# One attention layer of a four-layer graph network: attended products put off by two pairs and placed beside the scores

## The chip, the core and the metric

The kernel runs on one core of a Trainium2 chip. TensorE (PE in the profile, PEld for its weight loads), VectorE (DVE), ScalarE (ACT), GpSimd (POOL) and SyncE (SP) each run their own program and meet at semaphores. The metric is the device time of one launch in microseconds; lower is better.

## The reference

Input x is 64 graphs of 128 nodes with 256 features, with one 128x128 adjacency. Four layers follow, each x = x + layer(relu(layernorm(x))). The change touches the last, a masked attention of 8 heads of 32 features:

```python
q = (x @ Wq + bq).reshape(b, n, H, HD)      # likewise k, v
scores = jnp.einsum('bqhd,bkhd->bhqk', q, k) / jnp.sqrt(jnp.float32(HD))
scores = scores + (1.0 - adj)[None, None, :, :] * -1000000000.0
attn = jax.nn.softmax(scores, axis=-1)
out = jnp.einsum('bhqk,bkhd->bqhd', attn, v).reshape(b, n, d)
return out @ Wo + bo
```

## The kernel before

All of x stays in SBUF. The 64 graphs are worked on as 32 pairs (PAIRS = 32), layer after layer. In the last layer every engine runs a list of steps named period(p); the lists are software pipelines written out by hand, so a step of one pair stands beside steps of the pairs next to it, and the order of the calls in period is the order on the engine. A head belongs to one of R = 4 row groups r (32 features) and one of C = 2 chunks c, so a group r holds four 128x128 score blocks of a pair: two graphs by two chunks.

What happens to pair p, with its lines:

- PE turn: transposes the normalised x (L143). ACT relu_high (L1167) and DVE low_h (L1278) split its ReLU in a high and a low part.
- PE project_q, project_k, project_v: 12 matmuls each (L365). ACT copy_q (L1173), DVE copy_k (L1254) and copy_v (L1261) bring the results to SBUF. The projections of k and v land in the PSUM banks of score groups 0 and 1, so scores waits for both copies.
- PE scores (L1096): 16 matmuls with 32 rows of contraction, four groups of rows; the trace counts two passes of each.
- DVE mask_max(p, r) (L1267 and L1270): adds the mask, takes the negated maximum. ACT exponentials(p, r) (L1181): four instructions with their sums. DVE inverse(p, r) (L1274), POOL divide(p, r) (L1233).
- PE turn_prob(p, r) (L1104): four transposes into one of two banks PT; ACT copy_pT (L1188) brings them to probT.
- PE attend (L1114): 16 matmuls with full contraction and 32 columns of output, into bank OT. ACT copy_o (L1193) makes the high part, DVE low_o (L1283) the low part. PE project_o (L365 with wo), whose result YY is the same bank as OT. DVE update (L1290) adds it to x, SP stores the pair (L1341).
- Statistics for pair p + 3: DVE moments, mean_variance (L107, L114) and root_argument (nmean L120, vare L121); POOL inverse_root and centre (L132, L336). POOL add_bias (L1228) adds the output bias to x.

attend(p - 1) stands in period p behind project_k, project_o(p - 2) behind scores. On DVE, update(p - 2) stands early in the period, behind low_h; at the end come copy_v(p + 1), root_argument, low_o(p - 1). Waits that matter here: attend(p) needs all four copy_pT of its pair and update(p - 1) (x_done); scores(p) needs v_ready of pair p; low_o needs copy_o; project_o needs low_o. The loops run two pairs a turn on PE and DVE, one on ACT.

Of the kernel before, what the change touches and what calls it, by code (L numbers as in the profile page):

```python
# [14 lines left out]
def gnn_stack_kernel(nc, x, adj, w):  # L15


    GRAPHS, N, D = x.shape
    PAIRS = GRAPHS // 2
# [10 lines left out]
    with ExitStack() as ctx:  # L30
        def sb(name, shape, dt=F32):
            return ctx.enter_context(nc.sbuf_tensor(name, shape, dt))
# [52 lines left out]
        prob = sb("prob", [128, R, 2 * C, N])  # L85
        probT = sb("probT", [128, R, 2 * C, N])
        qT = sb("qT", [128, C, 2, N])
# [297 lines left out]
        with nc.Block() as block:  # L385
# [671 lines left out]
            QUAD = 2 * C  # L1057
            valb = [val, val1]
            nmax = [small[:, QUAD * r:QUAD * (r + 1)] for r in range(R)]
# [3 lines left out]
            def has(p, low, high=PAIRS):  # L1063
                return not isinstance(p, int) or low <= p < high

            @block.tensor
            def _(pe):
                def turn(p, b):
                    pe.wait_ge(xn_ready, p + 1)
                    pe.wait_ge(q_ready, since(p))  # L1070
                    transposes(TQ, xnb[b]).then_inc(tr_done, 1)

# [34 lines left out]
                def attend(p, b):  # L1107
                    pe.wait_ge(pt_ready, R * p + R)
                    pe.wait_ge(x_done, since(p))
                    for g in range(2):  # L1110
                        for c in range(C):
                            for r in range(R):
                                h = c * R + r
                                ins = nc.tensor.matmul(OT[HD * r:HD * (r + 1), (g * C + c) * N:(g * C + c + 1) * N],  # L1114
                                                       valb[b][:, g, HD * h:HD * (h + 1)], probT[:, r, g * C + c, :],
                                                       start=True, stop=True)
                    ins.then_inc(o_done, 1)
# [8 lines left out]
                def period(p, b):  # L1126
                    if has(p, 0):
                        scores(p)
                    if has(p, 2, PAIRS + 2):
                        project_o(p - 2)  # L1130
                    if has(p, 1, PAIRS + 1):
                        turn_prob(p - 1, 2)
                        turn_prob(p - 1, 3)
                    if has(p, 0, PAIRS - 1):
                        project_q(p + 1)
                        project_k(p + 1)
                    if has(p, 1, PAIRS + 1):
                        attend(p - 1, 1 - b)
                    if has(p, 0):
                        turn_prob(p, 0)  # L1140
                    if has(p, 0, PAIRS - 1):
                        project_v(p + 1)
                    if has(p, 0, PAIRS - 2):
                        turn(p + 2, b)
                    if has(p, 0):
                        turn_prob(p, 1)
# [6 lines left out]
                pe.wait_ge(l2_x_done, PAIRS)  # L1153
                period(0, 0)
                period(1, 1)
                with pe.Fori(1, PAIRS // 2 - 1) as j:
                    period(2 * j, 0)
                    period(2 * j + 1, 1)
                for p in range(PAIRS - 2, PAIRS + 2):
                    period(p, p % 2)  # L1160

            @block.scalar
            def _(act):
# [20 lines left out]

                def copy_pT(p, r):
                    act.wait_ge(pt_done, R * p + r + 1)
                    act.wait_ge(o_done, since(p))
                    nc.scalar.copy(probT[:, r, :, :].rearrange("p i n -> p (i n)"), PT[r % 2][:, :]).then_inc(pt_ready, 1)  # L1188

# [4 lines left out]

                def period(p):
                    if has(p, 1, PAIRS + 1):
                        copy_pT(p - 1, 1)
                    if has(p, 0, PAIRS - 1):
                        relu_high(p + 1)
                    if has(p, 0):  # L1200
                        exponentials(p, 0)
                    if has(p, 1, PAIRS + 1):
                        copy_pT(p - 1, 2)
                        copy_pT(p - 1, 3)
                    if has(p, 0):
                        exponentials(p, 1)
                    if has(p, 0, PAIRS - 1):
                        copy_q(p + 1)
                    if has(p, 0):
                        exponentials(p, 2)  # L1210
                    if has(p, 1, PAIRS + 1):
                        copy_o(p - 1)
                    if has(p, 0):
                        copy_pT(p, 0)
                        exponentials(p, 3)

                copy_q(0)
                period(0)
                with act.Fori(1, PAIRS - 1) as p:
                    period(p)  # L1220
                period(PAIRS - 1)
                period(PAIRS)

# [26 lines left out]
            def _(dve):  # L1250
# [7 lines left out]
                def copy_v(p, b):  # L1258
                    dve.wait_ge(v_done, p + 1)
                    dve.wait_ge(o_done, since(p - 1))  # L1260
                    nc.vector.tensor_tensor(valb[b][:, :, 0:D], VV[:, :].rearrange("p (g d) -> p g d", g=2),  # L1261
                                            rows[:, 1:2, :].to_broadcast([128, 2, D]), ALU.add).then_inc(v_ready, 1)
# [30 lines left out]
                def period(p, b):  # L1293
# [4 lines left out]
                    if has(p, 0, PAIRS - 1):  # L1298
                        low_h(p + 1)
                    if has(p, 2, PAIRS + 2):  # L1300
                        update(p - 2)
                    if has(p, 0):
                        mask_max(p, 1)
                        inverse(p, 0)
                        mask_max(p, 2)
                    if has(p, 0, PAIRS - 1):
# [4 lines left out]
                    if has(p, 0, PAIRS - 3):  # L1311
                        dve.wait_ge(xn_ready, p + 2)
                        moments(dve, p + 3, dstep, 1 - b)
                        mean_variance(dve, p + 3, dstep, 1 - b)
                    if has(p, 0):
                        inverse(p, 2)
                    if has(p, 0, PAIRS - 1):
                        copy_v(p + 1, 1 - b)
                    if has(p, 0, PAIRS - 3):
                        root_argument(dve, p + 3, dstep, stats_ready, 1 - b)  # L1320
                    if has(p, 1, PAIRS + 1):
                        low_o(p - 1)

# [3 lines left out]
                layer_norm_stats(dve, 2, dstep, stats_ready, 0)  # L1327
                period(0, 0)
                period(1, 1)
                with dve.Fori(1, PAIRS // 2 - 2) as j:  # L1330
                    period(2 * j, 0)
                    period(2 * j + 1, 1)
                for p in range(PAIRS - 4, PAIRS + 2):
                    period(p, p % 2)

# [31 lines left out]
```

## Time and profile before

| | us |
|---|---|
| median of 3 runs | 810.2 (810.06 to 811.39) |
| the profiled execution | 807.73 |
| its span, first to last instruction | 805.5 |
| busy: PE, DVE, ACT, POOL | 747.7, 716.3, 592.6, 491.5 |
| mean granted TensorE clock | 0.987 of full |

The time of the profiled execution is the span and 2.2 us around it. The last layer begins at about 450 us. In its steady part PE, DVE and ACT are all over nine tenths busy, so the page alone doesn't say which sets the pace; the waits and the order in time do. In the timeline a row gives the start, the length, the engine, the line, what it writes and reads, how many instructions were merged, and in brackets how long the engine was idle before it and what ended that.

### The profile page before, as it was taken

The page shows a single profiled execution, that of the slowest core. Times are in us where ns is not written, and L with a number is a line of the kernel's source. Part 1 is how long each engine was busy: PE and PEld are TensorE (multiplying, and loading weights), DVE is VectorE, ACT ScalarE, POOL GpSimd, SP SyncE. Part 2 cuts the span into 40 slices and gives each one's busy share as a digit, 9 for nine tenths or more (in the row PEclk, how much of TensorE's full clock was granted, in tenths as well). Part 3 has the DMA queues.
Part 4 walks back from the last instruction along what each step waited for, and adds up shares of the span by engine and source line. Part 5 has one row for each costly group of instructions (what it writes and reads, how often), then busy time and mean ns, then how long its engine had stood idle before and what let it go on. Part 6 is the DMA issues. An engine that isn't in the chain of part 4 may idle for free.

```text
span 805.5 us, 23074 instructions
## 1 busy us (share of the span) xinstructions
PE 747.7 (93%) x7065; PEld 684.9 (85%) x7065; DVE 716.3 (89%) x1941; ACT 592.6 (74%) x1928; POOL 491.5 (61%) x615
## 2 busy tenths in 40 slices
PE   4999999998889888887999889999999999999995
PEld 3899999998667666666999779999999999999994
DVE  4688888886899999998999889999999999999984
ACT  2544555454877887875766489999999999999995
POOL 1355545554566666667888466666667666666653
PEclk8999999999999999999999999999999999999998
DMA  6333300000000000000000000000000000000001
GB/s 192 92 92 91 91 0 0 0 0 0 2 1 0 0 0 0 0 1 1 1 0 0 1 15 27 25 15 26 26 26 26 26 26 26 26 13 26 26 28 39
DMA packets 21642, 19.91 MB, mean 25 GB/s; under 512 B 2416, under 2 KB 21616, under 8 KB 21616
## 3 DMA queue, kind: packets, MB, share of 16 engines
q1 hardware_dynamic: 19440, 18.16, 7.2%
q10 hardware_dynamic: 2176, 1.44, 0.6%
q8 instruction: 11, 0.18, 0.1%
q14 instruction: 15, 0.12, 0.1%
HBM read 11.21 MB, written 8.39 MB: 24 GB/s over the span
## 4 chain that ended last, share of the span: by engine, by line
PE 33%; ACT 28%; DVE 17%; issue 11%; POOL 8%; ACTq 1%; DVEq 0%; POOLq 0%
ACT prob L1181 20%; PE bank L365 18%; ACT probT L1188 5%; POOL xs L801 5%; PE bank L417 3%; PE bank L430 3%; DVE stats L107 3%; PE bank L345 3%; DVE wide L1267 3%; DVE small L1270 3%; POOL rstd L132 3%; PE bank L143 2%; DVE tT L840 2%; PE bank L425 1%; DVE prob L845 1%
## 5 line engine op out<-in xcount | busy, mean ns | idle before, releaser
L1181 ACT ACTIVATE prob<-wide,small 128x128 f32<-128x128 f32 x512 | 199.5, 395 | 27.2 <-DVE small L1270 27.2
L1233 POOL TENSOR_TENSOR prob<-prob,small 128x512 f32<-128x512 f32 x128 | 133.2, 1041 | 109.3 <-DVE small L1274 107.4
L132 POOL TENSOR_TENSOR rstd<-vare,mhalf 128x2 f32<-128x2 f32 x128 | 88.8, 694 | 99.5 <-DVE vare L121 99.5
L107 DVE BATCH_NORM_STATS2 stats<-xs 128x6 f32 (+1 forms) x256 | 95.2, 413 | 7.9 <-DMA xs<-in_x_dram 5.0
L1181 ACT ACTIVATION_READ_ACCUMULATOR prob<-wide,small 128x1 f32 x512 | 98.4, 192 | 0.0
L1270 DVE TENSOR_REDUCE small<-wide 128x4 f32<-128x512 f32 x128 | 87.8, 686 | 4.4
L1267 DVE TENSOR_TENSOR wide<-bank,mbias 128x512 f32<-128x512 f32 x128 | 86.1, 672 | 1.3 <-PE bank L1096 1.0
L329 ACT ACTIVATE xn<-xs,shift,rstd 128x256 f32 (+1 forms) x128 | 70.3, 601 | 16.2 <-POOL shift L138 16.2
L1104 PE MATMUL bank<-ident,prob 128*128 128x128 f32 x512 | 74.4, 279 | 1.2 <-POOL prob L1233 1.2
L1188 ACT COPY probT<-bank 128x512 f32<-128x512 f32 x128 | 70.7, 576 | 1.7 <-PE bank L1104 1.7
L1104 PEld LDWEIGHTS bank<-ident,prob 128*128 128x128 f32 x512 | 58.0, 142 | 7.8 <-issue 6.1
L355 PE MATMUL bank<-w,hT 128*128 128x257 f32 x256 | 62.5, 387 | 0.8 <-ACT hT L724 0.8
L143 PE MATMUL bank<-ident,xn 128*128 128x128 f32 x384 | 58.0, 274 | 0.5 <-DVE xn L1031 0.5
L365 PE MATMUL bank<-hTs,wq 128*128 128x256 f32 x384 | 54.2, 290 | 3.1 <-DVE hTs L1278 3.1
L365 PE MATMUL bank<-wo,oTs 128*128 128x256 f32 x384 | 54.9, 292 | 2.2 <-DVE oTs L1283 2.2
L355 PEld LDWEIGHTS bank<-w,hT 128*128 128x128 f32 x256 | 49.3, 194 | 8.8 <-ACT hT L724 1.3
L365 PE MATMUL bank<-w,yTs 128*128 128x256 f32 x384 | 54.1, 290 | 1.8 <-DVE xs L998 1.1
L519 POOL TENSOR_TENSOR relsq<-relm 128x256 f32<-128x256 f32 x32 | 22.1, 689 | 54.2 <-PE bank L430 54.2
L365 PE MATMUL bank<-wv0T,hTs 128*128 128x256 f32 x384 | 53.9, 289 | 1.1 <-DVE oTs L579 1.1
L365 PE MATMUL bank<-hTs,m_qk 128*128 128x256 f32 x384 | 52.4, 286 | 2.5 <-PEq L189 1.9
L365 PEld LDWEIGHTS bank<-wo,oTs 128*128 128x128 f32 x384 | 48.1, 190 | 6.3 <-DVE oTs L1283 2.7
L365 PE MATMUL bank<-wv,hTs 128*128 128x256 f32 x384 | 53.2, 287 | 0.0
(132 smaller groups left out, 1969.6 us busy)
## 6 DMA issues: line engine op xcount, KB each, us to landing
out_dram<-xs SPq DMA_DIRECT2D x32, 256.0 KB, 2.1
xs<-in_x_dram SPq DMA_DIRECT2D x28, 256.0 KB, 2.7
xs<-in_x_dram ACTq DMA_DIRECT2D x1, 768.0 KB, 7.6
xs<-in_x_dram ACTq DMA_DIRECT2D x1, 256.0 KB, 4.2
wq<-in_L_gnn_Wq_dram SPq DMA_DIRECT2D x1, 256.0 KB, 3.9
wk<-in_L_gnn_Wk_dram SPq DMA_DIRECT2D x1, 256.0 KB, 4.6
wv<-in_L_gnn_Wv_dram SPq DMA_DIRECT2D x1, 256.0 KB, 7.3
w<-in_L_gnn_W_dram SPq DMA_DIRECT2D x1, 256.0 KB, 8.2
```

The lines of the kernel that those rows point to most:

```text
L107: ins = nc.vector.bn_stats(stats[:, b, g, :], x_of(p, g))
L132: nc.gpsimd.tensor_tensor(rstd[:, b, :], vare[:, b, :], mhalf[:, :], ALU.pow).then_inc(rstd_ready, 1)
L143: ins = nc.tensor.transpose(pe_ps[:, c * 2 * N + g * N:c * 2 * N + (g + 1) * N], src[:, g, c * 128:(c + 1) * 128], ident[:, :])
L329: ins = nc.scalar.activation(dst[:, g, :], x_of(p, g), ACT.Relu, bias=shift[:, b, g:g + 1], scale=rstd[:, b, g:g + 1])
L355: ins = nc.tensor.matmul(ps_g, hT[:, c, g, :], weight[:, c, :], start=(c == 0), stop=(c == C - 1))
L365: ins = nc.tensor.matmul(ps, lhsT(a, c), rhs(b, c), start=(n == 0), stop=(n == len(terms) - 1))
L1104: ins = nc.tensor.transpose(PT[r % 2][:, i * N:(i + 1) * N], prob[:, r, i, :], ident[:, :])
L1181: ins = nc.scalar.activation(prob[:, r, i, :], wide[:, r, i, :], ACT.Exp, bias=nmax[r][:, i:i + 1], accum_out=rsum[r][:, i:i + 1])
L1188: nc.scalar.copy(probT[:, r, :, :].rearrange("p i n -> p (i n)"), PT[r % 2][:, :]).then_inc(pt_ready, 1)
L1233: nc.gpsimd.tensor_tensor(prob[:, r, :, :], prob[:, r, :, :], rinv[r].unsqueeze(2).to_broadcast([128, QUAD, N]), ALU.mult).then_inc(prob_r ...
L1267: nc.vector.tensor_tensor(wide[:, r, :, :], SS[r][:, :].rearrange("p (i n) -> p i n", i=QUAD), mbias_quad, ALU.add).then_inc(s_masked, 1)
L1270: nc.vector.tensor_reduce(nmax[r], wide[:, r, :, :], AX_X, ALU.max, negate=True).then_inc(nmax_ready, 1)
```

## The change

- attend(p - 2) now stands in period p directly behind scores(p); project_o(p - 2) moves behind project_k(p + 1).
- probT gets two buffers, the values four (val2, val3 are added); copy_pT waits for the attended products of one pair earlier, copy_v of two pairs earlier than before.
- ACT: copy_o(p - 2) stands behind exponentials(p, 0); before, copy_o(p - 1) stood behind exponentials(p, 2).
- DVE: low_o(p - 2) stands behind inverse(p, 0), update(p - 2) near the end; root_argument and update now stand ahead of copy_v(p + 1), which is last.
- The loops run four pairs a turn on PE and DVE, two on ACT.

No instruction of arithmetic is added or taken away. The diff, without the loop headers:

```diff
@@ -83,7 +83,8 @@
         rnorm = sb("rnorm", [128, 2])
         wide = sb("wide", [128, R, 2 * C, N])
         prob = sb("prob", [128, R, 2 * C, N])
-        probT = sb("probT", [128, R, 2 * C, N])
+        probT = [sb(f"probT{b}", [128, R, 2 * C, N]) for b in range(2)]
+        val2, val3 = sb("val2", [128, 2, D + 1]), sb("val3", [128, 2, D + 1])
         qT = sb("qT", [128, C, 2, N])
         kT = sb("kT", [128, C, 2, N])
         small = sb("small", [128, 64])
...
@@ -1055,7 +1056,7 @@
             SS, PT, OT, TQ = bank[0:4], bank[4:6], bank[6], bank[7]
             KK, VV, YY = SS[0], SS[1], OT
             QUAD = 2 * C
-            valb = [val, val1]
+            valb = [val, val1, val2, val3]
             nmax = [small[:, QUAD * r:QUAD * (r + 1)] for r in range(R)]
             rsum = [small[:, 16 + QUAD * r:16 + QUAD * (r + 1)] for r in range(R)]
             rinv = [small[:, 32 + QUAD * r:32 + QUAD * (r + 1)] for r in range(R)]
...
@@ -1112,7 +1113,7 @@
                             for r in range(R):
                                 h = c * R + r
                                 ins = nc.tensor.matmul(OT[HD * r:HD * (r + 1), (g * C + c) * N:(g * C + c + 1) * N],
-                                                       valb[b][:, g, HD * h:HD * (h + 1)], probT[:, r, g * C + c, :],
+                                                       valb[b][:, g, HD * h:HD * (h + 1)], probT[b % 2][:, r, g * C + c, :],
                                                        start=True, stop=True)
                     ins.then_inc(o_done, 1)
 
...
@@ -1127,15 +1128,15 @@
                     if has(p, 0):
                         scores(p)
                     if has(p, 2, PAIRS + 2):
-                        project_o(p - 2)
+                        attend(p - 2, (b + 2) % 4)
                     if has(p, 1, PAIRS + 1):
                         turn_prob(p - 1, 2)
                         turn_prob(p - 1, 3)
                     if has(p, 0, PAIRS - 1):
                         project_q(p + 1)
                         project_k(p + 1)
-                    if has(p, 1, PAIRS + 1):
-                        attend(p - 1, 1 - b)
+                    if has(p, 2, PAIRS + 2):
+                        project_o(p - 2)
                     if has(p, 0):
                         turn_prob(p, 0)
                     if has(p, 0, PAIRS - 1):
...
@@ -1182,44 +1183,45 @@
                                                    accum_out=rsum[r][:, i:i + 1])
                     ins.then_inc(exp_done, 1)
 
-                def copy_pT(p, r):
+                def copy_pT(p, r, b):
                     act.wait_ge(pt_done, R * p + r + 1)
-                    act.wait_ge(o_done, since(p))
-                    nc.scalar.copy(probT[:, r, :, :].rearrange("p i n -> p (i n)"), PT[r % 2][:, :]).then_inc(pt_ready, 1)
+                    act.wait_ge(o_done, since(p - 1))
+                    nc.scalar.copy(probT[b][:, r, :, :].rearrange("p i n -> p (i n)"), PT[r % 2][:, :]).then_inc(pt_ready, 1)
 
                 def copy_o(p):
                     act.wait_ge(o_done, p + 1)
                     act.wait_ge(y_done, since(p))
                     nc.scalar.copy(oTs[0][:, :, :, :].rearrange("p g c n -> p (g c n)"), OT[:, :]).then_inc(o_high_ready, 1)
 
-                def period(p):
+                def period(p, b):
                     if has(p, 1, PAIRS + 1):
-                        copy_pT(p - 1, 1)
+                        copy_pT(p - 1, 1, 1 - b)
                     if has(p, 0, PAIRS - 1):
                         relu_high(p + 1)
                     if has(p, 0):
                         exponentials(p, 0)
+                    if has(p, 2, PAIRS + 2):
+                        copy_o(p - 2)
                     if has(p, 1, PAIRS + 1):
-                        copy_pT(p - 1, 2)
-                        copy_pT(p - 1, 3)
+                        copy_pT(p - 1, 2, 1 - b)
+                        copy_pT(p - 1, 3, 1 - b)
                     if has(p, 0):
                         exponentials(p, 1)
                     if has(p, 0, PAIRS - 1):
                         copy_q(p + 1)
                     if has(p, 0):
                         exponentials(p, 2)
-                    if has(p, 1, PAIRS + 1):
-                        copy_o(p - 1)
-                    if has(p, 0):
-                        copy_pT(p, 0)
+                        copy_pT(p, 0, b)
                         exponentials(p, 3)
 
...
@@ -1257,7 +1259,7 @@
 
                 def copy_v(p, b):
                     dve.wait_ge(v_done, p + 1)
-                    dve.wait_ge(o_done, since(p - 1))
+                    dve.wait_ge(o_done, since(p - 3))
                     nc.vector.tensor_tensor(valb[b][:, :, 0:D], VV[:, :].rearrange("p (g d) -> p g d", g=2),
                                             rows[:, 1:2, :].to_broadcast([128, 2, D]), ALU.add).then_inc(v_ready, 1)
 
...
@@ -1297,11 +1299,12 @@
                         mask_max(p, 0)
                     if has(p, 0, PAIRS - 1):
                         low_h(p + 1)
-                    if has(p, 2, PAIRS + 2):
-                        update(p - 2)
                     if has(p, 0):
                         mask_max(p, 1)
                         inverse(p, 0)
+                    if has(p, 2, PAIRS + 2):
+                        low_o(p - 2)
+                    if has(p, 0):
                         mask_max(p, 2)
                     if has(p, 0, PAIRS - 1):
                         copy_k(p + 1)
...
@@ -1310,28 +1313,28 @@
                         mask_max(p, 3)
                     if has(p, 0, PAIRS - 3):
                         dve.wait_ge(xn_ready, p + 2)
-                        moments(dve, p + 3, dstep, 1 - b)
-                        mean_variance(dve, p + 3, dstep, 1 - b)
+                        moments(dve, p + 3, dstep, 1 - b % 2)
+                        mean_variance(dve, p + 3, dstep, 1 - b % 2)
                     if has(p, 0):
                         inverse(p, 2)
+                    if has(p, 0, PAIRS - 3):
+                        root_argument(dve, p + 3, dstep, stats_ready, 1 - b % 2)
+                    if has(p, 2, PAIRS + 2):
+                        update(p - 2)
                     if has(p, 0, PAIRS - 1):
-                        copy_v(p + 1, 1 - b)
-                    if has(p, 0, PAIRS - 3):
-                        root_argument(dve, p + 3, dstep, stats_ready, 1 - b)
-                    if has(p, 1, PAIRS + 1):
-                        low_o(p - 1)
+                        copy_v(p + 1, (b + 1) % 4)
 
```

## Rows read from the trace of the kernel before

**Rows 1.** Waits in 470 to 780 us: who waited for what, us in total, times, longest

```profile
ACT prob L1181 <- DVE small L1270: 21.6, 29, 0.8
...
DVE small L1274 <- ACT prob L1181: 9.8, 30, 0.9
```

**Rows 2.** Timeline of one pair, VectorE (start us, length us, engine, line, operation)

```profile
646.83 0.69 DVE L1267 TENSOR_TENSOR wide<-bank,mbias 128x512 f32<-128x512 f32 x1
...
648.15 0.68 DVE L1278 SCALAR_TENSOR_TENSOR hTs<-bank,hTs 128x512 fp32r<-128x512 f32 x1
...
648.75 0.68 DVE L1290 TENSOR_TENSOR xs<-bank,xs 128x512 f32 x1
...
650.75 0.66 DVE L1267 TENSOR_TENSOR wide<-bank,mbias 128x512 f32<-128x512 f32 x1
...
655.06 0.14 DVE L1274 RECIPROCAL small<-small 128x4 f32<-128x4 f32 x1
...
655.12 0.68 DVE L1261 TENSOR_TENSOR val<-bank,rows 128x512 f32<-128x512 f32 x1
...
655.71 0.64 DVE L120 TENSOR_SCALAR nmean<-mv 128x2 f32<-128x2 f32 x1
...
657.42 0.69 DVE L1267 TENSOR_TENSOR wide<-bank,mbias 128x512 f32<-128x512 f32 x1
```

**Rows 3.** Timeline of the same pair, ScalarE

```profile
648.35 0.40 ACT L1181 ACTIVATE prob<-wide,small 128x128 f32<-128x128 f32 x1 [0.79 <-DVE small L1270]
...
649.91 1.04 ACT L1188 COPY probT<-bank 128x512 f32<-128x512 f32 x2
...
654.58 0.19 ACT L1181 ACTIVATION_READ_ACCUMULATOR prob<-wide,small 128x1 f32 x1
```

**Rows 4.** Timeline of the same pair, TensorE

```profile
648.89 1.70 PE L365 MATMUL bank<-hTs,wq 128*128 128x256 f32 x12
...
650.42 1.60 PE L365 MATMUL bank<-hTs,wk 128*128 128x256 f32 x12
...
652.96 0.42 PEld L1104 LDWEIGHTS bank<-ident,prob 128*128 128x128 f32 x4 [0.20 <-issue]
...
656.01 1.01 PEld L1096 LDWEIGHTS bank<-kT,qT 32*128 32x128 f32 x32 [0.32 <-issue]
```

**Rows 5.** Timeline of pair 0 to 1: copy_v, scores, mask_max

```profile
463.76 0.66 DVE L1261 TENSOR_TENSOR val<-bank,rows 128x512 f32<-128x512 f32 x1
...
464.65 1.01 PEld L1096 LDWEIGHTS bank<-kT,qT 32*128 32x128 f32 x32 [1.49 <-issue]
...
464.68 1.17 PE L1096 MATMUL bank<-kT,qT 32*128 32x128 f32 x32 [1.28 <-DVE val L1261]
...
465.91 0.69 DVE L1267 TENSOR_TENSOR wide<-bank,mbias 128x512 f32<-128x512 f32 x1 [0.78 <-PE bank L1096]
```

**Rows 6.** Timeline of the same pair as group 2, GpSimd

```profile
653.91 1.30 POOL L1228 TENSOR_TENSOR xs<-xs,rows 128x512 f32<-128x512 f32 x1
...
655.28 1.04 POOL L1233 TENSOR_TENSOR prob<-prob,small 128x512 f32<-128x512 f32 x1
```

**Rows 7.** Timeline of the last pairs and the end

```profile
783.44 1.17 PE L1096 MATMUL bank<-kT,qT 32*128 32x128 f32 x32 [0.55 <-DVE val L1261]
...
797.79 1.08 PE L1114 MATMUL bank<-probT,val 128*32 128x128 f32 x32 [0.67 <-ACT probT L1188]
...
798.93 0.58 ACT L1193 CAST oTs<-bank 128x512 fp32r<-128x512 f32 x1 [1.20 <-PE bank L1114]
...
799.55 0.69 DVE L1283 TENSOR_TENSOR oTs<-bank,oTs 128x512 fp32r<-128x512 f32 x1 [3.42 <-ACT oTs L1193]
...
802.04 0.69 DVE L1290 TENSOR_TENSOR xs<-bank,xs 128x512 f32<-128x512 f32 x1 [1.79 <-PE bank L365]
```

**Rows 8.** Lines 120 and 121: durations ns min/median/max, first and last start

```profile
L120 DVE TENSOR_SCALAR nmean<-mv x128: 152/224/655, 6.1 to 762.0; 128x2 f32<-128x2 f32 x128
...
L121 DVE TENSOR_SCALAR vare<-mv x128: 152/155/164, 6.2 to 762.6; 128x2 f32<-128x2 f32 x128
```

More of the change, by code:

```diff
@@ L1070, in turn @@
                     pe.wait_ge(q_ready, since(p))
-                    transposes(TQ, xnb[b]).then_inc(tr_done, 1)
+                    transposes(TQ, xnb[b % 2]).then_inc(tr_done, 1)
                 def project_q(p):
@@ L1153, in _ @@
                 pe.wait_ge(l2_x_done, PAIRS)
[L1154 to L1160, printed above, removed]
+                for p in range(4):
+                    period(p, p)
+                with pe.Fori(1, PAIRS // 4 - 1) as j:
+                    for i in range(4):
+                        period(4 * j + i, i)
+                for p in range(PAIRS - 4, PAIRS + 2):
+                    period(p, p % 4)
             @block.scalar
@@ L1210, in period @@
                         exponentials(p, 2)
-                    if has(p, 1, PAIRS + 1):
-                        copy_o(p - 1)
-                    if has(p, 0):
-                        copy_pT(p, 0)
+                        copy_pT(p, 0, b)
                         exponentials(p, 3)
                 copy_q(0)
[L1218 to L1222, printed above, removed]
+                period(0, 0)
+                period(1, 1)
+                with act.Fori(1, PAIRS // 2 - 1) as j:
+                    period(2 * j, 0)
+                    period(2 * j + 1, 1)
+                for p in range(PAIRS - 2, PAIRS + 2):
+                    period(p, p % 2)
             @block.gpsimd
@@ L1327, in _ @@
                 layer_norm_stats(dve, 2, dstep, stats_ready, 0)
[L1328 to L1332, printed above, removed]
+                for p in range(4):
+                    period(p, p)
+                with dve.Fori(1, PAIRS // 4 - 1) as j:
+                    for i in range(4):
+                        period(4 * j + i, i)
                 for p in range(PAIRS - 4, PAIRS + 2):
-                    period(p, p % 2)
+                    period(p, p % 4)
             @block.sync
```

## The prediction

> **What bounds the kernel now.** I read three views, in this order. First the table of waits over the steady stretch of the last layer [rows 1]: the only two waits that recur once a pair are the exponentials on ACT for the negated maximum from DVE (29 times, 21.6 us, so 0.74 us a pair) and the reciprocals on DVE for the exponentials (30 times, 9.8 us). ACT and DVE wait for each other; nobody is shown waiting for PE, although PE is as full as they are. Then the timeline of one pair [rows 2 to 4]. I call m the start of mask_max(p, 0). One pair lasts 657.42 - 646.83 = 10.59 us there [rows 2], and the mean over 30 pairs, from scores(1) at 464.68 (its weight load is in [rows 5]) to scores(31) at 783.44 [rows 7], is 10.63 us. The circle is: the last exponential of a pair ends, DVE can take inverse(p-1, 3), then mask_max(p, 0); ACT starts exp 0 at m + 1.52 (648.35 - 646.83) [rows 2, 3] and is then full to the end of the pair.
>
> Last, the second circle, which no table names: copy_v, scores, mask_max. copy_v starts at 655.12 and runs about 0.67 us, so it ends near 655.8, and the scores' weight load starts at 656.01 [rows 2, 4]. The row puts 0.32 us of idle down to "issue". But in pair 1 the same load is idle 1.49 us, and it starts 0.89 us after copy_v's start (463.76 to 464.65) [rows 5], as it does here (655.12 to 656.01). PE had nothing else left there, so it waits for v_ready in both; the wait is real and stands hidden in "issue". From copy_v's start to the next mask_max is 2.15 us when nothing else holds it (463.76 to 465.91) [rows 5]. In the steady pair copy_v starts at m + 8.29 [rows 2], so this circle is 8.29 + 2.15 = 10.44 us long against the real 10.59. Its slack is 0.15 us. Any delay of copy_v beyond that lengthens every pair.
>
> **The change part by part.** *PE.* attend (1.0 us: project_k starts at 650.42, a projection takes 1.53 to the next, and the transposes behind attend load at 652.96 [rows 4]) moves up behind scores; project_o (12 matmuls, like project_q, so 1.53) moves down behind project_k. project_q waits for low_h: 648.15 + 0.68 = 648.83, q at 648.89 [rows 2, 4], so it can't start earlier. Hence the stretch from q to the last transposes grows by some 0.5 us less what a change of array shape costs. PE was through with its other loads at 656.01 - 0.32 = 655.69, i.e. m + 8.9, and would be at m + 9.4. This is under the m + 10.3 found below, so it costs nothing, and what PE saves gives nothing either. For the shapes: the weight load after attend is idle 0.20 us [rows 4]; of four changes of shape a pair one goes, since the scores (32 rows) and the attended products (32 columns) are themselves two shapes. I price that at 0 to 0.3 us a pair on PE, hidden.
>
> The Trainium skill (TensorEngine Tiling (Array Packing), Key Properties) says that a change of tiling mode, not merely of tile, drains the array. The 0.20 us agree. By that rule alone the change would give 0.20 x 30 = 6 us if PE set the time; it is the first rival below.
>
> *ACT.* copy_o(p-2) goes between exp 0 and the copies of turned probabilities, the same instruction, none added. It starts no earlier than m + 1.52 + (649.91 - 648.35) = m + 3.08 and lasts 0.57 (798.93) [rows 3, 7], so it ends at m + 3.65. Its own input, attend, ends before m + 1. Exp 2 then ends at most 0.57 later than before relative to exp 0: m + 1.52 + (654.58 + 0.19 - 648.35) + 0.57 = m + 8.51.
>
> *DVE.* Here is the cost. (a) low_o takes update's place early in the pair. They are alike (PSUM and SBUF in, 512 wide; from one such operation to the next takes 0.60, as low_h to update [rows 2]), so the exchange is free, but low_o now needs copy_o. DVE reaches it at m + 3.32 (650.75 - 646.83 less 0.60) [rows 2]; copy_o ends at m + 3.65 and low_o follows 0.05 later (798.93 + 0.57 = 799.50, then 799.55) [rows 7]. So DVE stands 0.37 us, and behind it are queued mask_max 2, copy_k, mask_max 3 and all the rest. (b) update moves in front of copy_v: 0.60 us (copy_v to the next is 0.59 [rows 2]). (c) root_argument moves in front of copy_v. It costs 0.59 + more where it stands now, since nmean lasts 0.64 us instead of 0.15; its end, 656.35, is that of divide on POOL, 655.28 + 1.04 = 656.32 [rows 2, 6]. At the new place, 0.06 us behind inverse(p, 2), the divide which that reciprocal releases has not begun (POOL starts 0.22 behind it). Free, two such small operations cost 0.14 us (0.06 to 0.08 each to the next; shortest durations 0.15 in [rows 8]). Bounds 0.14 and 1.1 (a whole divide first); I take 0.14. (d) The waits ahead of inverse(p, 2): DVE reaches it at m + 8.23 + 0.37 = 8.60, behind exp 2's 8.51, so it adds nothing.
>
> Copy_v now starts at m + 8.29 + 0.37 + 0.14 + 0.60 = m + 9.40; project_v is over by then (q at m + 2.06, three projections 1.53 apart, four transposes of 0.42 together, a fourth projection and its tail of 0.2: m + 8.8, from [rows 4]). With 2.15 for copy_v, scores and the way to mask_max the pair is **11.55 us** instead of 10.63: +0.92. The old cover is gone: root_argument, low_o and inverse 3 used to run on DVE during the scores; now only inverse 3 does, and DVE and ACT both stand while the scores run.
>
> *Buffers.* The second probT and four values relax waits on o_done that show in no table; worth nothing here.
>
> *Sum.* Pairs 2 to 28: 27 x 0.92 = 24.9 us. Pairs 29 and 30 have no statistics; there exp 2 holds inverse(p, 2) until m + 8.5, and the pair is 8.5 + 0.1 + 0.6 + 2.15 = 11.3, some 0.7 more: 1.3 us. Pairs 0 and 1 have no low_o or update: only root_argument, 0.3 us. *The end:* now 18.6 us pass from scores(31) to the last update, and 4.25 from attend(31) to it [rows 7]. With the lag, attend(31) must wait for update(30), and that for the whole line attend, copy_o, low_o, project_o of pair 30, which itself waits for project_o behind turn_prob(31, 3). Laying these in line gives update(30) at 13.4 to 14.0 after the last m, attend(31) at 14.25 and update(31) at 18.5 against 17.2: +1.3 us (bounds 0 and 3). In all 24.9 + 1.3 + 0.3 + 1.3 = 27.8 us. The profiled execution took 807.7 us and would take 835.5. The median of the runs is 0.3% above the profiled one, so I give 810.2 + 27.8 = **838 us**.
>
> Bounds of the terms: without the 0.37 us the sum falls by 10 us, so 828; rounding in the six small steps is 2 us, so 826. With root_argument held for a whole divide in each pair, +1.0 x 28 = 28 us, so 866.
>
> **Rivals.** *PE is the bound (faster).* PE is idle for only some tenths of a us a pair, and its 0.32 us before scores and 0.20 after attend could both be changes of shape. Then three instead of four save 0.20 us x 30 = 6 us: 804. It decides if scores don't wait for copy_v. Against it: the 1.49 us of idle at the same place, with the same 0.89 us behind copy_v [rows 5]. Chance 0.06.
>
> *The ACT and DVE circle absorbs it (no change).* If DVE still reached mask_max before the last exponential was through, the pair would stay 10.6 and the time 810 to 812. It needs copy_v to be at most 0.15 us later; the instructions put before it come to 1.1 us. Chance 0.05.
>
> *POOL gets in ahead of root_argument (slower still).* The margin is small: add_bias (653.91 + 1.30 = 655.21 [rows 6], so m + 8.38, with the 0.37 m + 8.75) still runs when nmean comes at m + 8.66, and the divide can start at m + 8.82. If the divide slips in before vare, update and copy_v wait 1.0 us more: 12.6 us a pair, 866. For it: nmean held today. Against: vare never took over 0.164 us in 128 [rows 8]. Chance 0.14. The Trainium skill (SBUF — State Buffer, Who interferes with whom) says that a VectorE tensor_scalar in a two-port mode and a GpSimd instruction exclude each other for a whole instruction, whoever comes first. By that rule nmean ahead of the divide is free; behind it the 866 holds. The 656.35 against 656.32 agrees.
>
> **How the numbers follow.** My case, slower by 3.4%, has 0.75. The range 826 to 866 takes in all slower cases and leaves out the two others, 0.11, and some error of the sum. A difference under about 0.2% can't be told from none by a measurement of this kernel. Faster 0.06, same 0.05, slower 0.89.
>
> **What would show it.** Right: in the steady pairs DVE is idle before mask_max(p, 0) for roughly 1 us, released by the scores on PE (L1096), and ACT before exp 0 for about 1.5 us; DVE is idle before low_o 0.3 to 0.4 us, released by copy_o; nmean is short; PE is idle before scores some 0.8 us behind copy_v; scores to scores is 11.5 us. Wrong: scores start long after copy_v's end, or nmean or vare lasts over 0.6 us at the new place, or DVE still waits for exp 3 and not for scores.

## The result

The changed kernel is slower: median 845.2 us (6 runs) against 810.8 us of the kernel before (6 runs), a ratio of 1.0418 with a 95% interval of 1.0389 to 1.0447. That is 34 us, where 27.8 were forecast; 838 was named and 826 to 866 was the range. One of the six runs of the changed kernel took 1207 us at a granted clock of 0.557; the ratio leaves it out, and the median of the other five is 845.1 us. The profiled execution took 847.4 us, its span is 845.7 us.

The changed kernel's lines are one or two higher than before: scores L1097, attend L1115, copy_o L1194, copy_v L1263, mask_max L1269 and L1272, low_o L1285, update L1292, exponentials L1182, reciprocals L1276. Its table of waits over the steady part of the last layer (who waited for whom, us in total, times, longest) answers [rows 1]:

```profile
PEld bank L1097 <- issue: 39.2, 29, 2.3
DVE wide L1269 <- PE bank L1097: 34.0, 30, 1.5
PE bank L1097 <- DVE val L1263: 33.0, 29, 2.0
PEld bank L366 <- DVE hTs L1280: 13.2, 30, 1.3
...
DVE small L1276 <- ACT prob L1182: 8.6, 29, 0.8
```

Two new waits stand near the top that before had not: DVE's mask_max for the scores (30 times, 34.0 us) and the scores for copy_v (29 times, 33.0 us). They are the two halves of one circle. The timeline of one pair, VectorE, answers [rows 2]; m is now 646.85:

```profile
646.85 0.69 DVE L1269 TENSOR_TENSOR wide<-bank,mbias 128x512 f32<-128x512 f32 x1 [1.15 <-PE bank L1097]
...
648.18 0.68 DVE L1280 SCALAR_TENSOR_TENSOR hTs<-bank,hTs 128x512 fp32r<-128x512 f32 x1
...
650.53 0.69 DVE L1285 TENSOR_TENSOR oTs<-bank,oTs 128x512 fp32r<-128x512 f32 x1 [0.27 <-ACT oTs L1194]
651.14 0.68 DVE L1269 TENSOR_TENSOR wide<-bank,mbias 128x512 f32<-128x512 f32 x1
...
655.46 0.15 DVE L1276 RECIPROCAL small<-small 128x4 f32<-128x4 f32 x1
...
655.59 0.17 DVE L121 TENSOR_SCALAR nmean<-mv 128x2 f32<-128x2 f32 x1
...
655.66 0.17 DVE L122 TENSOR_SCALAR vare<-mv 128x2 f32<-128x2 f32 x1
...
655.80 0.69 DVE L1292 TENSOR_TENSOR xs<-bank,xs 128x512 f32 x1
...
656.41 0.68 DVE L1263 TENSOR_TENSOR val<-bank,rows 128x512 f32<-128x512 f32 x1
...
657.32 0.18 DVE L1276 RECIPROCAL small<-small 128x4 f32<-128x4 f32 x1 [0.23 <-ACT prob L1182]
...
658.68 0.69 DVE L1269 TENSOR_TENSOR wide<-bank,mbias 128x512 f32<-128x512 f32 x1 [1.18 <-PE bank L1097]
```

The same pair on TensorE and ScalarE, for [rows 3, 4]:

```profile
647.62 0.86 PEld L1105 LDWEIGHTS bank<-ident,prob 128*128 128x128 f32 x8 [0.20 <-issue]
...
648.37 0.40 ACT L1182 ACTIVATE prob<-wide,small 128x128 f32<-128x128 f32 x1 [1.92 <-PE bank L1105]
...
648.91 1.49 PEld L366 LDWEIGHTS bank<-hTs,wq 128*128 128x128 f32 x12 [0.43 <-DVE hTs L1280]
...
649.93 0.57 ACT L1194 CAST oTs<-bank 128x512 fp32r<-128x512 f32 x1
...
657.32 1.01 PEld L1097 LDWEIGHTS bank<-kT,qT 32*128 32x128 f32 x32 [1.36 <-issue]
...
657.35 1.17 PE L1097 MATMUL bank<-kT,qT 32*128 32x128 f32 x32 [1.15 <-DVE val L1263]
...
658.45 0.81 PEld L1115 LDWEIGHTS bank<-probT,val 128*32 128x32 f32 x32
```

The pair lasts 658.68 - 646.85 = 11.83 us, against 10.59 in [rows 2]. copy_v starts at m + 9.56 (it was 8.29); low_o waits 0.27 us for copy_o; VectorE stands 1.18 us before mask_max, TensorE's weight loads 1.36 us before the scores. ScalarE's wait before exp 0, put down to TensorE here, is 1.92 us where it was 0.79 [rows 3].

Where the 40.2 us between the two spans lie, by the starts of the scores: up to scores(0), in code that did not change, 2.3 us (454.23 to 456.57); pair 0, 1.7 us (10.45 to 12.18); pairs 1 to 30, 34.1 us (10.63 to 11.76 on average); from scores(31) to the last update 2.1 us (18.6 to 20.7). In pair 0 TensorE stands 2.1 us for low_h, and 0.6 us behind the end of this its clock falls to the lower level of 1.2 GHz. Two stretches of the changed kernel (busy time of each engine with count, then the granted clock, before the DMA's share):

```profile
459.90:464.30 4.40, 4.40 (x24) 4.40 (x25) 2.54 (x5) 4.13 (x21) 1.04 (x1) 0.61 0.00 0
...
839.20:842.20 3.00, 2.91 (x12) 2.62 (x12) 0.03 (x1) 0.00 (x0) 0.00 (x0) 0.52 0.00 0
```

project_q and project_k of pair 1 took 2.47 and 2.38 us there, against 1.70 and 1.60 at the full clock. The second stretch is the last project_o: 2.91 us instead of 1.70. The fall in pair 0 does not come with the new order: of the 12 profiled executions behind this document it is missing in that of the kernel before alone, and e5 below, in which only VectorE's order differs from before, has it. The end of the kernel before has a stretch at half clock of its own:

```profile
462.10:465.50 3.40, 3.40 (x19) 3.40 (x17) 1.65 (x4) 3.14 (x16) 1.04 (x1) 0.50 0.00 0
```

```profile
794.10:797.50 3.40, 3.01 (x15) 2.61 (x13) 0.87 (x2) 1.73 (x5) 1.04 (x1) 0.50 0.07 24
```

The first is e5 in pair 0, the second the kernel before in its last pairs. The profiled execution of before (807.7 us) was also shorter than each of its six runs of this comparison, and that of the changed kernel the longest of its five. That is the likely reason why the spans differ by 40 and the medians by 34, but the other executions have no trace that would show it.

### The profile page after: what moved, and what is told of

Same layout as the page of the kernel before. It is cut to its first block, busy times and chain, and to the rows that moved or that the text cites. A ratio compares the mean times of both kernels' runs of the same rounds, so it can differ in the third digit from the quotient of the medians.

```text
span 845.7 us, 22865 instructions
## 1 busy us (share of the span) xinstructions
PE 751.2 (89%) x7065; PEld 687.1 (81%) x7065; DVE 711.2 (84%) x1941; ACT 592.5 (70%) x1928; POOL 491.1 (58%) x615
## 4 chain that ended last, share of the span: by engine, by line
PE 36%; DVE 29%; issue 13%; POOL 10%; ACT 8%; DVEq 1%; ACTq 0%; POOLq 0%
PE bank L366 18%; DVE wide L1269 7%; ACT prob L1182 6%; DVE stats L108 5%; PE bank L1097 5%; POOL xs L802 4%; PE bank L418 3%; DVE small L1272 3%; PE bank L431 3%; PE bank L346 3%; DVE val L1263 3%; POOL rstd L133 2%; DVE kT L1256 2%; ACT oTs L1194 2%; PE bank L144 2%
## 5 line engine op out<-in xcount | busy, mean ns | idle before, releaser
L1182 ACT ACTIVATE prob<-wide,small 128x128 f32<-128x128 f32 x512 | 200.2, 400 | 63.5 <-PE bank L1105 47.5
L1269 DVE TENSOR_TENSOR wide<-bank,mbias 128x512 f32<-128x512 f32 x128 | 87.1, 681 | 34.9 <-PE bank L1097 34.9
L1182 ACT ACTIVATION_READ_ACCUMULATOR prob<-wide,small 128x1 f32 x512 | 101.4, 198 | 0.0
L1272 DVE TENSOR_REDUCE small<-wide 128x4 f32<-128x512 f32 x128 | 87.8, 686 | 4.4
L1097 PE MATMUL bank<-kT,qT 32*128 32x128 f32 x1024 | 37.6, 282 | 36.1 <-DVE val L1263 36.1
L1097 PEld LDWEIGHTS bank<-kT,qT 32*128 32x128 f32 x1024 | 32.2, 186 | 42.9 <-issue 42.9
L366 PEld LDWEIGHTS bank<-hTs,wq 128*128 128x128 f32 x384 | 48.4, 191 | 15.5 <-DVE hTs L1280 15.5
L366 PE MATMUL bank<-wo,oTs 128*128 128x256 f32 x384 | 52.7, 287 | 3.8 <-DVE oTs L1285 3.8
```

What stands on the lines that cost most here:

```text
L366: ins = nc.tensor.matmul(ps, lhsT(a, c), rhs(b, c), start=(n == 0), stop=(n == len(terms) - 1))
L1097: ins = nc.tensor.matmul(SS[r][:, (g * C + c) * N:(g * C + c + 1) * N], qT[rows_r, c, g, :], kT[rows_r, c, g, :], start=True, stop=True)
L1182: ins = nc.scalar.activation(prob[:, r, i, :], wide[:, r, i, :], ACT.Exp, bias=nmax[r][:, i:i + 1], accum_out=rsum[r][:, i:i + 1])
L1269: nc.vector.tensor_tensor(wide[:, r, :, :], SS[r][:, :].rearrange("p (i n) -> p i n", i=QUAD), mbias_quad, ALU.add).then_inc(s_masked, 1)
L1272: nc.vector.tensor_reduce(nmax[r], wide[:, r, :, :], AX_X, ALU.max, negate=True).then_inc(nmax_ready, 1)
```

## The experiments

Two theories. **A**, that of the prediction: copy_v comes late on VectorE, the scores wait for it, and mask_max for the scores; the order on VectorE costs the time. **B**: TensorE's new order costs it, project_q standing for low_h (0.4 us a pair in the table of waits) and project_o ahead of project_v. All edits are in the last layer; "pair" is the mean from scores(1) to scores(31) of the profiled execution.

| run | median us | ratio to before, 95% | pair us |
|---|---|---|---|
| before | 810.8 | | 10.63 |
| changed | 845.2 | 1.039 to 1.045 | 11.76 |
| e1_copyv_first | 818.3 | 1.007 to 1.012 | 10.91 |
| e2_update_late | 826.2 | 1.018 to 1.022 | 11.13 |
| e3_root_late | 838.3 | 1.031 to 1.036 | 11.56 |
| e4_lowo_late | 846.5 | 1.043 to 1.047 | 11.76 |
| e5_before_copyv_last | 832.2 | 1.023 to 1.029 | 11.37 |
| e6_attend_first | 855.3 | 1.053 to 1.057 | 12.07 |
| e8_v_early_split | 809.9 | 0.998 to 1.002 | 10.65 |
| e9_v_early_only | 809.3 | 0.996 to 0.999 | 10.61 |
| e10_loop_unrolled | 839.0 | 1.032 to 1.037 | 11.60 |
| e12_lag_tuned | 815.3 | 1.002 to 1.007 | 10.80 |

### Undoing the order on VectorE, step by step

```diff
 # e1_copyv_first, in VectorE's period of the changed kernel
                         inverse(p, 2)
+                    if has(p, 0, PAIRS - 1):
+                        copy_v(p + 1, (b + 1) % 4)
                     if has(p, 0, PAIRS - 3):
                         root_argument(dve, p + 3, dstep, stats_ready, 1 - b % 2)
                     if has(p, 2, PAIRS + 2):
                         update(p - 2)
-                    if has(p, 0, PAIRS - 1):
-                        copy_v(p + 1, (b + 1) % 4)
```

> The changed kernel with one edit: on VectorE copy_v(p+1) stands directly behind inverse(p,2) again, ahead of root_argument and update. TensorE, ScalarE, lag and buffers stay as changed. Theory A (the time is lost because copy_v comes late and scores wait for it): copy_v starts at m + 8.7 and the way to the next mask_max takes 2.2 to 2.3, so a pair takes 10.9 to 11.0 us instead of 11.8 and the time is 818 to 822 us. Rival B (the time is lost in TensorE's new order: project_q waits for low_h, and project_o stands ahead of project_v): the order on VectorE hardly matters, over 838 us.

Measured 818.3 us, as A has it. Theory B is out for the bulk of the loss: TensorE's order, the lag and the buffers are all still there, and 27 of the 34 us are gone. The 7 or 8 us left are the changed kernel's rest. Timeline of this kernel, one pair:

```profile
642.77 0.69 DVE L1269 TENSOR_TENSOR wide<-bank,mbias 128x512 f32<-128x512 f32 x1 [0.27 <-PE bank L1097]
...
646.45 0.69 DVE L1285 TENSOR_TENSOR oTs<-bank,oTs 128x512 fp32r<-128x512 f32 x1 [0.26 <-ACT oTs L1194]
...
651.45 0.66 DVE L1263 TENSOR_TENSOR val<-bank,rows 128x512 f32<-128x512 f32 x1
...
652.02 0.65 DVE L121 TENSOR_SCALAR nmean<-mv 128x2 f32<-128x2 f32 x1
...
652.33 1.01 PEld L1097 LDWEIGHTS bank<-kT,qT 32*128 32x128 f32 x32 [0.43 <-issue]
...
653.69 0.69 DVE L1269 TENSOR_TENSOR wide<-bank,mbias 128x512 f32<-128x512 f32 x1 [0.27 <-PE bank L1097]
```

copy_v starts at m + 8.68 (651.45 - 642.77) and mask_max 2.24 us behind it: the same circle still holds the pair, at 10.92 us. It is 0.39 us later than in [rows 2], about as much as low_o's wait for copy_o pushes the steps behind it (in the changed kernel mask_max 2 starts at m + 4.29, in [rows 2] at m + 3.92). And nmean is back at 0.65 us: behind a copy_v it meets the divide on GpSimd again.

```diff
 # e2_update_late; here and in e3 the conditions ahead of the calls are left out
                         root_argument(dve, p + 3, dstep, stats_ready, 1 - b % 2)
-                        update(p - 2)
                         copy_v(p + 1, (b + 1) % 4)
+                        update(p - 2)
 # e3_root_late
-                        root_argument(dve, p + 3, dstep, stats_ready, 1 - b % 2)
                         update(p - 2)
                         copy_v(p + 1, (b + 1) % 4)
+                        root_argument(dve, p + 3, dstep, stats_ready, 1 - b % 2)
```

> The changed kernel with one edit: update(p-2) stands behind copy_v instead of ahead of it; root_argument stays ahead. Theory A: 0.61 to 0.68 us off in each of 29 pairs, 18 to 20 us, so 825 to 828 us. Rival B: within 3 us of the changed kernel, 842 to 846.

> The changed kernel with one edit: root_argument stands behind copy_v instead of ahead of it; update stays ahead. Theory A: root_argument costs 0.2 us a pair where it stands, 27 pairs, so 5 us are won, 840 us; nmean then runs into the divide on POOL again, but in the shadow of the scores. A rival in which nmean is held for a whole divide at the changed place would win 15 us or more here, under 832.

Measured 826.2 and 838.3 us. Update's place is worth 0.63 us a pair (11.76 - 11.13), root_argument's 0.20 (11.76 - 11.56), together 0.83, and e1 has 0.85: the two add, as two steps in a row on one path do. The rival in which nmean is held for a whole divide is out.

```diff
 # e4_lowo_late
-                    if has(p, 2, PAIRS + 2):
-                        low_o(p - 2)
                     if has(p, 0):
                         mask_max(p, 2)
+                    if has(p, 2, PAIRS + 2):
+                        low_o(p - 2)
```

> The changed kernel with one edit: low_o(p-2) stands behind mask_max(p,2) instead of ahead of it, where copy_o is long done. Theory A: VectorE's wait of 0.35 us for copy_o goes in each of 29 pairs, 10 us, so 835 us; project_o starts 0.3 us later, which may take a part of it back by a later project_v. Rival: the wait is hidden behind another (exp 2 or project_v), then 843 to 846.

Measured 846.5 us: nothing is won, and the rival in it was right, though it named other waits. VectorE in that kernel (copy_k, the reciprocal of group 1, the mask of group 3):

```profile
650.16 0.69 DVE L1256 TENSOR_TENSOR kT<-bank,bk 128x512 f32<-128x512 f32 x1
651.11 0.18 DVE L1276 RECIPROCAL small<-small 128x4 f32<-128x4 f32 x1 [0.26 <-ACT prob L1182]
651.20 0.68 DVE L1269 TENSOR_TENSOR wide<-bank,mbias 128x512 f32<-128x512 f32 x1
```

The step from copy_k to the mask was 0.68 us in the changed kernel and is 1.04 here (651.20 - 650.16), with inverse(p, 1) standing for exp 1. Exp 1 ends where it did, at m + 6.16 in both kernels, and copy_o stands ahead of it on ScalarE; in the kernel before, without copy_o there, it ends at m + 5.7. So I put the 0.36 us down to copy_o's place on ScalarE: low_o's wait was only the first one to show it, and taken away it turns up 2.5 us later as another.

### Doing it alone, on the kernel before

```diff
 # e5_before_copyv_last, on the kernel before
-                    if has(p, 0, PAIRS - 1):
-                        copy_v(p + 1, 1 - b)
                     if has(p, 0, PAIRS - 3):
                         root_argument(dve, p + 3, dstep, stats_ready, 1 - b)
                     if has(p, 1, PAIRS + 1):
                         low_o(p - 1)
+                    if has(p, 0, PAIRS - 1):
+                        copy_v(p + 1, 1 - b)
```

> The kernel before with one edit: on VectorE copy_v(p+1) stands last in the period, behind root_argument and low_o(p-1). No lag, no new buffer, TensorE and ScalarE as before. Theory A: copy_v starts at m + 9.1 instead of 8.3, a pair takes 11.3 us instead of 10.6, and the time is 828 to 833 us: most of the change's loss without the change. Rival B (TensorE's order): within 3 us of before, 808 to 814.

Measured 832.2 us. Without any lag, buffer or new order on TensorE, the late copy_v alone costs 22 us, at 0.74 us a pair.

### Is the shared stretch worth anything on TensorE?

```diff
 # e6_attend_first, in TensorE's period of the changed kernel
+                    if has(p, 2, PAIRS + 2):
+                        attend(p - 2, (b + 2) % 4)
                     if has(p, 0):
                         scores(p)
-                    if has(p, 2, PAIRS + 2):
-                        attend(p - 2, (b + 2) % 4)
```

> The changed kernel with one edit: attend(p-2) stands ahead of scores(p) instead of behind it, so it runs while TensorE waits for copy_v. Theory A: TensorE is not what sets the pair, 843 to 847 us, the pair stays 11.8; the idle time ahead of scores shrinks by 1 us and that ahead of project_q grows by as much. Rival C (the order of the two shapes of the array matters for the time): more than 4 us either way.

Measured 855.3 us, 10 slower than the changed kernel. Theory A missed, and the number is in rival C's range. TensorE and the two VectorE steps around it:

```profile
646.83 0.69 DVE L1292 TENSOR_TENSOR xs<-bank,xs 128x512 f32 x1
...
647.43 0.68 DVE L1263 TENSOR_TENSOR val<-bank,rows 128x512 f32<-128x512 f32 x1
...
647.63 0.84 PEld L1115 LDWEIGHTS bank<-probT,val 128*32 128x32 f32 x32 [0.63 <-issue]
...
648.67 0.98 PEld L1097 LDWEIGHTS bank<-kT,qT 32*128 32x128 f32 x32 [0.20 <-issue]
...
649.78 0.86 PEld L1105 LDWEIGHTS bank<-ident,prob 128*128 128x128 f32 x8
...
650.02 0.69 DVE L1269 TENSOR_TENSOR wide<-bank,mbias 128x512 f32<-128x512 f32 x1 [1.47 <-PE bank L1097]
...
652.08 1.49 PEld L366 LDWEIGHTS bank<-hTs,wq 128*128 128x128 f32 x12 [1.45 <-DVE hTs L1280]
```

attend(p - 2) needs x_done, the update of pair p - 3, since YY and OT are one bank, and that update now stands late, directly ahead of copy_v (646.83). So attend can't fill the idle time; it starts behind update (647.63), ends after copy_v, and pushes the scores to 648.67, 1.24 us behind copy_v's start instead of 0.91. I had left that wait out. Rival C is right in part too: of the 1.04 us from attend's first load to the scores' first, 0.20 are idle time between the two shapes, and they lie on the path here.

The loads show what a change of shape costs. The view puts idle time in brackets only above some 0.15 us, so the shorter gaps have to be worked out. TensorE's loads in the kernel before, the same pair as in [rows 4]:

```profile
650.30 1.51 PEld L365 LDWEIGHTS bank<-hTs,wk 128*128 128x128 f32 x12
...
651.95 0.81 PEld L1114 LDWEIGHTS bank<-probT,val 128*32 128x32 f32 x32
...
653.35 1.50 PEld L365 LDWEIGHTS bank<-wv,hTs 128*128 128x128 f32 x12
...
657.15 1.49 PEld L365 LDWEIGHTS bank<-wo,oTs 128*128 128x128 f32 x12
```

Where the shape stays there is no gap: the transposes' loads end at 652.96 + 0.42 = 653.38 and project_v's begin at 653.35. At each of the four changes there is one: 0.14 us ahead of attend (650.30 + 1.51 = 651.81, then 651.95), 0.20 behind it, 0.13 behind the scores (656.01 + 1.01 = 657.02, then 657.15), and 0.17 ahead of the scores where no copy holds them (e9 below). In the changed kernel it is 0.12 from the scores to attend (657.32 + 1.01 = 658.33, then 658.45), and 0.20 behind attend again. So scores and attended products don't share a shape, but side by side they make three changes of four. From these gaps I estimate that TensorE saves about 0.2 us a pair, which the time can't show as TensorE isn't what holds the pair. The Trainium skill (TensorEngine Tiling (Array Packing), Key Properties) has every change of mode drain the array; the gap at each of the four changes agrees.

### Why the pair was 0.2 us longer than the sum

```diff
 # e10_loop_unrolled, VectorE of the changed kernel
-                with dve.Fori(1, PAIRS // 4 - 1) as j:
-                    for i in range(4):
-                        period(4 * j + i, i)
-                for p in range(PAIRS - 4, PAIRS + 2):
+                for p in range(4, PAIRS + 2):
                     period(p, p % 4)
```

> The changed kernel with VectorE's loop of the last layer written out, so that its waits are on constants for every pair; all else as changed. In the trace of the changed kernel mask_max starts 0.16 us behind the end of the scores inside the loop and 0.06 outside, and update and copy_v start late too: if that is the loop, a pair falls from 11.8 to 11.6 for 24 pairs and the time is 839 to 842 us. If not, 843 to 847.

Measured 839.0 us, pair 11.60, so 0.16 us a pair and 6 us in all. The scores and the mask behind them in this kernel:

```profile
642.34 1.17 PE L1097 MATMUL bank<-kT,qT 32*128 32x128 f32 x32 [1.34 <-DVE val L1263]
...
643.58 0.69 DVE L1269 TENSOR_TENSOR wide<-bank,mbias 128x512 f32<-128x512 f32 x1 [1.28 <-PE bank L1097]
```

The mask starts 0.07 us behind the end of the scores (642.34 + 1.17 = 643.51). In the changed kernel's loop it is 0.16 (657.35 + 1.17 = 658.52, then 658.68), as its chain of work shows, with a register instruction of VectorE's queue (DVEq) between the two, which the chain of e10 hasn't:

```profile
645.51 1.21 PE bank L1097 x32
...
646.75 0.05 DVEq L1268
...
646.85 0.70 DVE wide L1269
```

### What would it take to gain?

```diff
 # e9_v_early_only, on the kernel before: TensorE, then VectorE
+                        project_v(p + 1)
                         attend(p - 1, 1 - b)
                         turn_prob(p, 0)
-                        project_v(p + 1)
...
                         moments(dve, p + 3, dstep, 1 - b)
+                        copy_v(p + 1, 1 - b)
                         mean_variance(dve, p + 3, dstep, 1 - b)
                         inverse(p, 2)
-                        copy_v(p + 1, 1 - b)
 # e8_v_early_split: e9 and, in mask_max(p, 0), between the mask and the maximum
+                        inverse(p - 1, 3)
 # e12_lag_tuned: e10 with the same on the changed kernel; on TensorE
+                        project_v(p + 1)
                         project_o(p - 2)
                         turn_prob(p, 0)
-                        project_v(p + 1)
```

> The kernel before with two edits: project_v(p+1) ahead of attend(p-1) on TensorE and copy_v(p+1) between moments and mean_variance on VectorE; inverse(p-1,3) stays ahead of mask_max(p,0). Theory A: the circle through copy_v falls to about 10.2 us but the one through the last exponential and inverse(p-1,3) holds the pair at 10.6: 808 to 812 us, no difference. Rival (copy_v is already what sets the kernel before): 0.2 us or more a pair, 804 or less.

> The kernel before with three edits that shorten both circles: project_v(p+1) stands ahead of attend(p-1) on TensorE; copy_v(p+1) stands between moments and mean_variance on VectorE; inverse(p-1,3) stands between the mask and the maximum of mask_max(p,0), so that the mask no longer waits for the last exponential. Theory A: neither circle holds the pair at 10.6 any more, TensorE's own work of 10.3 to 10.4 us does: 801 to 806 us. Rival: the later divide(p-1,3) or attend gives it back, 808 to 813.

> The changed kernel with four edits: project_v(p+1) ahead of project_o(p-2); copy_v(p+1) between moments and mean_variance; inverse(p-1,3) between the mask and the maximum of mask_max(p,0); VectorE's loop written out. The lag of two pairs and the shared stretch stay. Theory A: copy_v holds nothing any more, TensorE's circle from low_h over the scores to the next low_h does, 10.5 to 10.6 us a pair: 805 to 812 us, so the lag itself costs nothing and gives nothing. Rival (the lag costs by itself, in waits of attend or at the end): 818 or more.

Measured 809.3, 809.9 and 815.3 us. In e9 the circle through copy_v has over 0.4 us of slack and the pair is still 10.61: it was not what held the kernel before. VectorE now stands 0.90 us at the reciprocal for the last exponential, where it was 0.3:

```profile
645.69 0.68 DVE L1261 TENSOR_TENSOR val<-bank,rows 128x512 f32<-128x512 f32 x1
...
646.82 0.98 PEld L1096 LDWEIGHTS bank<-kT,qT 32*128 32x128 f32 x32 [0.17 <-issue]
...
648.27 0.18 DVE L1274 RECIPROCAL small<-small 128x4 f32<-128x4 f32 x1 [0.90 <-ACT prob L1181]
```

The median is 0.2% under that of before, at the edge of what can be told. In e8 neither circle holds, and the pair is 10.65 all the same; my 10.3 was too low and the rival came true, since the reciprocal that moved behind the mask makes divide(p-1, 3) later and TensorE's turn_prob(p-1, 3) stands 0.30 us for it:

```profile
642.78 0.46 PEld L1104 LDWEIGHTS bank<-ident,prob 128*128 128x128 f32 x4
...
643.54 0.42 PEld L1104 LDWEIGHTS bank<-ident,prob 128*128 128x128 f32 x4 [0.30 <-POOL prob L1233]
```

e12, with the lag, is 0.5% above before and 3 us above what I had expected. There the same turn_prob stands 0.65 us for divide, as project_o no longer stands ahead of it:

```profile
641.00 0.42 PEld L1105 LDWEIGHTS bank<-ident,prob 128*128 128x128 f32 x4 [0.20 <-issue]
...
642.07 0.42 PEld L1105 LDWEIGHTS bank<-ident,prob 128*128 128x128 f32 x4 [0.65 <-POOL prob L1235]
```

So 30 of the 34 us come back with the lag of two pairs and the shared stretch in place; by e10 some 6 of them are the loop written out, which the kernel before hasn't, so whether the lag by itself is free is not shown. I found no version that clearly beats the kernel before.

## Why the prediction was right, and where it was off

- **The circle through copy_v**: right. It was read from two rows (the 1.49 us of idle in pair 1, and the 0.32 put down to "issue" at the same distance behind copy_v). e1, e2, e3 and e5 move copy_v against its neighbours on VectorE and the pair follows.
- **Its slack**: 0.15 us forecast, about 0.04 by the runs. With the 2.27 us that the way from copy_v to mask_max takes inside the loop (2.26 in e5) this circle was 8.29 + 2.27 = 10.56 us long in the kernel before, against 10.60; e1 agrees, where copy_v is 0.39 us later and the pair 0.33 longer than in [rows 2]. The forecast was right in the order of the two circles, but they were nearer to each other than it had them.
- **update ahead of copy_v**: 0.60 forecast, 0.63 measured by e2.
- **root_argument ahead of copy_v**: 0.14 forecast, 0.20 by e3. nmean was free at its new place (0.17 us at 655.59), so the rival with GpSimd didn't come true in the steady pairs; it starts 0.13 behind the reciprocal and not 0.06, also in the written-out loop. The Trainium skill (SBUF — State Buffer, Who interferes with whom) agrees on the other side: in e1 the divide is under way first (651.61 + 1.04 = 652.65) and nmean takes 0.65 us and ends at 652.67.
- **low_o's wait**: right in place (low_o at m + 3.68, forecast 3.70) and in what it adds to the steps behind it (0.37 us; 0.27 of it shows as idle time), wrong in what stands behind it. I bounded the case without it at 10 us less; e4 shows 0, since exp 1, itself delayed by copy_o, would have held inverse(p, 1) by as much. The step that failed is the bound in the sum, where I tested only exp 2 against the shift and not exp 1. That the sum held here is partly luck: both waits end in the same place.
- **The way from copy_v to mask_max**: 2.15 forecast from pair 1, 2.27 measured. Pair 1 stands outside the loop; that row was the wrong one to take for pairs inside it. With update's 0.07 more this is the 0.18 us a pair which e10 wins back (11.83 to 11.65 in one pair, 11.76 to 11.60 on average), the largest part of what the sum was short.
- **The pairs without statistics**: 11.3 forecast, 11.3 measured for pair 29 (scores at 799.01 and 810.32).
- **TensorE**: m + 9.4 forecast for being ready, 9.1 measured (657.32 - 1.36 - 646.85), with 0.43 us of standing for low_h; hidden, as said. It is 0.25 us more than before, where 0.5 less the price of a change of shape was forecast. Its rival (TensorE is the bound) fell with e1 and e6.
- **The end**: 1.3 forecast, 2.1 measured. Attend(31) does wait for update(30), 0.88 us at 836.78. The last project_o lost 1.2 us to the half clock, but the end of the kernel before lost something to it too (794.10 to 797.50 above), and in e10 the end is 1.4 longer than before (20.0 against 18.6), so how much of the 2.1 is the clock stays open.

So the mechanism was right, and the sum was 6 us short by several small steps of 0.06 to 0.12 us a pair.

What stays open: the changed kernel with copy_v put back is still 7 us over the kernel before. By the timeline and by e4 most of the 0.39 us by which copy_v is later there comes from copy_o's place ahead of exp 1, but this isn't shown; a kernel with copy_o alone moved back was not run.

## What to carry to other kernels

When three engines are each over nine tenths busy, look for the circles that come back to the same instruction one iteration later and write down the length of each; here they were 10.60 us through the last exponential, 10.56 through copy_v and, as an estimate, 10.35 of TensorE's own (e8's 10.65 less the 0.30 it stands), and a step can be moved only as far as the slack of every circle on which it lies. A copy that frees a bank for the next iteration's first product belongs early enough for its circle to have slack (e9 shows that further forward gains nothing), and the end of the period was the worst place for it here, as VectorE then had little to do while the product ran. A wait that you remove is worth only the distance to the next one that ends on the same chain, so check all the waits behind it against the shift, not just the last.

## What the runs showed of the hardware

- Every change of shape left a gap of 0.12 to 0.20 us between TensorE's weight loads (0.20 behind products with 32 columns of output, 0.12 to 0.17 at the other three changes), where loads of one shape follow each other without one. Gaps of 0.14 us and less carry no bracket in the timeline.
- A VectorE instruction that waits for TensorE starts 0.16 us behind it inside the loop of the last layer, and 0.06 to 0.07 where the loop is written out. It costs only where the wait is real: 6 us here (839.0 against 845.2).
- In pair 0 TensorE stands 2.1 us for low_h in all 12 profiled executions. In 11 of them its clock falls to the 1.2 GHz level, from 0.4 us before to 0.9 us behind the end of this idle time (in the changed kernel a granted clock of 0.61 over 4.4 us); in that of the kernel before it stays at the full clock from there until 794.1 us.
